# Expert products on 32-column quarters of the TensorE array, gated rows turned by VectorE

## The chip, the core and the metric

The kernel runs on one core of a Trainium2 chip. The metric is the device time of one execution in microseconds (us), as the median of several runs; lower is better. TensorE is the matrix engine, VectorE, ScalarE and GpSimd (POOL) work on tiles in on-chip memory (SBUF) and in the accumulator memory (PSUM), and SyncE (SP) mostly issues transfers (DMA). All tensors here are float32.

## What is computed

A decoder of two layers over 2 x 2048 tokens of width 512: attention, cross-attention and a quantised feed-forward block, then a convolution layer, a cross-attention and a mixture of experts. The change concerns the last part, whose reference is

```python
x = inputs.reshape(b * s, e)                       # 4096 tokens, e = 512
gate_logits = jnp.einsum('te,ex->tx', x, gate_kernel)
weights, selected = jax.lax.top_k(gate_logits, TOP_K)     # 2 of 64 experts
weights = jax.nn.softmax(weights, axis=-1)
...
h0 = jax.lax.ragged_dot(sorted_x, w0, group_sizes)  # w0, w1: 64 x 512 x 1024
h1 = jax.lax.ragged_dot(sorted_x, w1, group_sizes)
inter = jax.nn.silu(h0) * h1
out_sorted = jax.lax.ragged_dot(inter, wo, group_sizes)   # wo: 64 x 1024 x 512
...
out = jnp.einsum('BKE,BK->BE', per_tok, weights)
```

Its result is added to the residual stream.

## The kernel before

The stages run one after the other; the last is `stage_experts` (L3233). The stage before it sorts the 8192 pairs of a token and an expert into tiles of G = 64 tokens with one expert each (partly filled where an expert's count is not a multiple of 64; some experts have no tile), and writes tables of the tokens of each tile and of the expert of each tile. The number of tiles is known only at run time, so each engine runs a loop `Fori` over four tiles (`rounds`, L3269 and after), with the last four tiles behind it. All engines meet by semaphores; nothing but the order written in each engine's block sets the order of its work.

Per tile c:

- SP (`load`) brings each expert's w0, w1 and wo (2 MB each) into a shelf of NBUF = 2 experts. The load of expert e waits until the last tile of expert e - 2 has taken its weights from the shelf, and SP issues the loads strictly in the order w0, w1, wo.
- VectorE `place` (L3376) copies w0 and w1 of the tile's expert from the shelf to `w_s[0]`, `w_s[1]`, ScalarE's `place` (L3425) copies wo to `w_s[2]`, for every tile. There is one such buffer for each, so a copy waits for the product of the tile before that reads it.
- ScalarE fetches the tile's token numbers (`st.fetch`, six small DMAs), VectorE makes indexes of them (L3358), POOL gathers the rows of x by indirect DMA (L3322), and VectorE turns them in 32x32 blocks into `xT`, 128 partitions x 4 blocks of the width x 64 tokens (`turn_x`, L3363).
- TensorE `up(c, p, which)` (L3474) multiplies with w0 (which = 0) or w1 (which = 1). A tile of 64 tokens is the stationary operand, 128 x 64, so one product fills half of the array's columns. The 1024 output columns are cut in Q = 2 halves of FQ = 512; half q goes to partitions q * 64 and after of PSUM bank `which`, for KD = 4 blocks of the width. So the two halves of the array work on the two halves of the output.
- ScalarE `silu` (L3430) makes g of bank 0, VectorE `gate` (L3382) multiplies it with bank 1 to h (128 x 512).
- TensorE `turn_h` (L3481) turns h by four transposes of 128x128 into bank 2, and ScalarE `keep_h` (L3435) copies it to `hT`.
- TensorE `down` (L3490) multiplies hT with wo: FC = 8 blocks, Q = 2 halves of DQ = 256 columns, into bank 4. VectorE scales the result by the token's weight (`y`, L3409), and POOL adds it to the output by indirect DMA (L3339).

The order on TensorE is up(c+1, w0), turn_h(c), up(c+1, w1), down(c). The order on VectorE is, for tile c: output index and weight, index(c+3), turn_x(c+2), place w0 (c+2), gate(c+1), place w1 (c+2), y(c). On ScalarE: fetch(c+4), silu(c+1), keep_h(c), place wo (c+1). xT, g, h and hT are double buffers.

In the traces each float32 matmul with a full stationary operand shows as two records of a weight load and a matmul.

Of the kernel before, what the change touches and what calls it, by code (L numbers as in the profile page):

```python
# [12 lines left out]
P = 128  # L13
# [2826 lines left out]
G = 64  # L2840
# [392 lines left out]
def stage_experts(nc, st, xn_d, table, out_d):  # L3233

    XH = G // LANES
    HJ = FQ // P
    FC = FF // P
    NS = NSLOT
    ident, part, own, shelf, consts_in, w_in = st.ident, st.part, st.own, st.shelf, st.consts_in, st.w_in
    raw, raw_in, raw_x, raw_x_in, entry, own_in = st.raw, st.raw_in, st.raw_x, st.raw_x_in, st.entry, st.own_in  # L3240
    with st:
# [6 lines left out]
        xT = st.sb("xT", [P, 2, KD, G])  # L3248
        g = st.sb("g", [P, 2, FQ])
        h = st.sb("h", [P, 2, FQ])  # L3250
        hT = st.sb("hT", [P, 2, FC, G])
        y = st.sb("y", [P, 4, DQ])
# [7 lines left out]
        h_done = st.count("h_done", 1)  # L3260
        t_mm = st.count("t_mm", 1)
        hT_done = st.count("hT_done", 1)
# [85 lines left out]
        def _(dve):  # L3348
            for s in (w_set[0], w_set[1], ix_done, out_set, xT_done, h_done, y_done):
                s.start(dve)  # L3350
# [27 lines left out]
            def gate(c, p):  # L3378
                dve.wait_ge(*g_done(c))
                dve.wait_ge(*up_mm[1](c))  # L3380
                dve.wait_ge(*t_mm(c - 2))
                dve.tensor_tensor(h[:, p % 2], g[:, p % 2], ps[:, 1, 0:FQ], ALU.mult).then_inc(h_done.sem, 1)  # L3382

            def first():
                for c in range(3):
                    index(0, c, c)
                for c in range(2):
                    turn_x(0, c, c)
                for c in range(2):
                    e, buf = owner(dve, c)  # L3390
                    for n in range(2):
                        place(n, c, e, buf)
                gate(0, 0)

            def main(i, c, p, left):
                aim(i, c, p)
                if left >= 3:
                    index(i + 1 if p else i, c + 3, (p + 3) % 4)
                if left >= 2:
                    turn_x(i + 1 if p >= 2 else i, c + 2, (p + 2) % 4)  # L3400
                    e, buf = owner(dve, c + 2)
                    place(0, c + 2, e, buf)
                if left >= 1:
                    gate(c + 1, p + 1)
                if left >= 2:
                    place(1, c + 2, e, buf)
                dve.wait_ge(*y_mm(c))
                dve.wait_ge(*out_set(c))
                dve.tensor_scalar(y[:, p, :], ps[:, 4, 0:DQ], wt[:, p:p + 1], None, ALU.mult).then_inc(y_done.sem, 1)  # L3409
# [4 lines left out]
        def _(act):  # L3414
            for s in (w_set[2], g_done, hT_done):
                s.start(act)
# [10 lines left out]
            def silu(c, p):  # L3427
                act.wait_ge(*up_mm[0](c))
                act.wait_ge(*h_done(c - 2))
                act.activation(g[:, p % 2], ps[:, 0, 0:FQ], ACT.Silu).then_inc(g_done.sem, 1)  # L3430

            def keep_h(c, p):
                act.wait_ge(*t_mm(c))
                act.wait_ge(*y_mm(c - 2))
                act.activation(hT[:, p % 2].rearrange("p (q j) t -> p j q t", j=HJ),  # L3435
                               ps[:, 2, 0:HJ * P].rearrange("p (j q t) -> p j q t", j=HJ, q=Q), ACT.Copy).then_inc(hT_done.sem, 1)

# [6 lines left out]
            def main(i, c, p, left):  # L3444
# [6 lines left out]
                if left >= 1:  # L3451
                    silu(c + 1, p + 1)
                keep_h(c, p)
                if left >= 1:
                    place(c + 1)
# [4 lines left out]
        def _(pe):  # L3460
            for s in (up_mm[0], up_mm[1], t_mm, y_mm):
                s.start(pe)
# [5 lines left out]
            def up(c, p, which):  # L3468
                pe.wait_ge(*w_set[which](c))
                pe.wait_ge(*xT_done(c))  # L3470
                pe.wait_ge(*(g_done, h_done)[which](c - 1))
                for k in range(KD):
                    for q in range(Q):
                        mm = pe.matmul(ps[q * G:(q + 1) * G, which, 0:FQ], xT[:, p % 2, k, :], wu[which][:, k, q * FQ:(q + 1) * FQ], start=k == 0, stop=k == KD - 1)  # L3474
                mm.then_inc(up_mm[which].sem, 1)

            def turn_h(c, p):
                pe.wait_ge(*h_done(c))
                pe.wait_ge(*hT_done(c - 1))
                for j in range(HJ):  # L3480
                    mm = pe.transpose(ps[:, 2, j * P:(j + 1) * P], h[:, p % 2, j * P:(j + 1) * P], ident[:, :])  # L3481
                mm.then_inc(t_mm.sem, 1)

            def down(c, p):
# [3 lines left out]
                for k in range(FC):  # L3488
                    for q in range(Q):
                        mm = pe.matmul(ps[q * G:(q + 1) * G, 4, 0:DQ], hT[:, p % 2, k, :], wd[:, k, q * DQ:(q + 1) * DQ], start=k == 0, stop=k == FC - 1)  # L3490
                mm.then_inc(y_mm.sem, 1)
# [5 lines left out]
            def main(i, c, p, left):  # L3497
                if left >= 1:
                    up(c + 1, p + 1, 0)
                turn_h(c, p)  # L3500
                if left >= 1:
                    up(c + 1, p + 1, 1)
# [64 lines left out]
def laid_out(inputs):  # L3567
# [8 lines left out]
    for n in ("L0_ffn_qweights", "L0_ffn_scales", "L0_ffn_lora_b"):  # L3576
        t[n] = t[n].transpose(0, 2, 1)
    t.update(shape_constants())
    return {n: np.ascontiguousarray(v) for n, v in t.items()}
# [13 lines left out]
```

## Time and profile before

| | |
|---|---|
| median of 3 runs | 5372.88 us (5367.45 to 5378.44) |
| span of the profiled execution | 5339.0 us |
| TensorE busy in it | 5071.4 us, 95%, 26,624 matmul records and as many weight loads |
| VectorE busy | 2763.7 us, 52% |
| ScalarE busy | 1731.5 us, 32% |
| POOL busy | 1689.6 us, 32% |
| granted TensorE clock, mean | 0.980 of full speed |

The span goes from the first to the last instruction of the profiled execution; the device time of a run holds some time ahead of it and behind it as well. The busy shares are means over stages with different limits. The expert stage begins at about 3460 us and lasts to the end. The views used below are: a table of busy times by stretch, one line's instructions, the chain of waits (the work that ended last, followed back from the end, printed in order of time), groups of instructions by line, and timelines. PE is TensorE's matmuls, PEld its weight loads, DVE VectorE, ACT ScalarE. "128*64 128x256" means a stationary operand of 128 rows and 64 columns and a moving one of 128 x 256.

### The profile page before, as it was taken

How to read it: one execution, taken by the hardware profiler on the slowest of the kernel's cores; microseconds unless marked ns; L12 is line 12 of the kernel's file. 1: busy time of each engine (PE TensorE's matmuls, PEld its weight loads, DVE VectorE, ACT ScalarE, POOL GpSimd, SP SyncE). 2: the span in 40 equal slices, each digit the busy share in tenths (PEclk: the TensorE clock that was granted, in tenths of full speed). 3: DMA queues.
4: the chain of work that ended last, by engine and by line, in shares of the span. 5: the costliest groups of instructions: out<-in, count | busy, mean ns of one | idle time of the engine just before them, and what ended most of it. 6: DMA issues, size and time to landing. Idle time of an engine off the chain costs nothing. (4 is left out here: it accounts for less than half of the span.)

```text
span 5339.0 us, 79687 instructions
## 1 busy us (share of the span) xinstructions
PE 5071.4 (95%) x26624; PEld 2768.0 (52%) x26624; DVE 2763.7 (52%) x4714; ACT 1731.5 (32%) x2238; POOL 1689.6 (32%) x1428
## 2 busy tenths in 40 slices
PE   9999989989999999899979999699999999999998
PEld 4444446668886566444444555534444444444444
DVE  4243237766653355455532565555555555555554
ACT  1011015544332200334321443134444444444433
POOL 1000005545553211000012222544444444444443
PEclk9999999989999999999999999899999999999999
DMA  1010021231111233799976022335545667789996
GB/s 58 8 46 10 8 85 48 70 98 32 24 32 64 101 107 132 178 219 211 222 204 218 25 72 77 104 101 150 180 146 185 212 218 250 264 290 332 383 383 233
DMA packets 493432, 771.88 MB, mean 145 GB/s; under 512 B 119505, under 2 KB 263638, under 8 KB 492708
## 3 DMA queue, kind: packets, MB, share of 16 engines
q1 hardware_dynamic: 377072, 723.32, 42.1%
q0 software_dynamic: 36160, 43.09, 4.1%
q10 hardware_dynamic: 79988, 2.67, 1.0%
q8 instruction: 129, 2.11, 0.2%
q14 instruction: 83, 0.68, 0.0%
HBM read 577.15 MB, written 116.26 MB: 130 GB/s over the span
## 5 line engine op out<-in xcount | busy, mean ns | idle before, releaser
L3474 PE MATMUL ex_ps<-ex_w,ex_xT 128*64 128x512 f32 x5248 | 1193.0, 597 | 13.3 <-DVE ex_w L3376 11.6
L3376 DVE COPY ex_w<-ex_shelf 128x4096 f32 x328 | 753.6, 2298 | 369.0 <-PE ex_ps L3474 235.1
L3425 ACT ACTIVATE ex_w<-ex_shelf 128x4096 f32 x164 | 593.4, 3618 | 888.8 <-PE ex_ps L3490 769.6
L3474 PEld LDWEIGHTS ex_ps<-ex_w,ex_xT 128*64 128x64 f32 x5248 | 366.7, 137 | 625.6 <-issue 588.7
L3490 PE MATMUL ex_ps<-ex_w,ex_hT 128*64 128x256 f32 x5248 | 596.9, 380 | 26.6 <-issue 22.7
L3322 POOL DMA_INDIRECT ex_x<-moe_xn,ex_ix x328 | 556.8, 1698 | 132.2 <-issue 98.7
L3339 POOL DMA_INDIRECT out<-ex_y,ex_ix_out x164 | 293.2, 1788 | 896.9 <-DVE ex_xT L3363 407.7
L3490 PEld LDWEIGHTS ex_ps<-ex_w,ex_hT 128*64 128x64 f32 x5248 | 384.1, 137 | 283.6 <-issue 120.3
L2766 POOL TENSOR_TENSOR go_xb<-go_xr,go_bias 128x2048 f32<-128x2048 f32 x8 | 38.2, 4774 | 719.5 <-DMA go_xr<-x 653.2
L3382 DVE TENSOR_TENSOR ex_h<-ex_g,ex_ps 128x512 f32<-128x512 f32 x164 | 112.6, 686 | 252.3 <-PE ex_ps L3474 214.9
L617 PE MATMUL at_ps<-at_xT,at_kT 128*128 128x512 f32 (+3 forms) x640 | 239.3, 529 | 1.6 <-ACT at_kT L511 1.6
L617 PEld LDWEIGHTS at_ps<-at_xT,at_kT 128*128 128x128 f32 x640 | 117.0, 191 | 121.5 <-issue 108.9
L1760 ACT ACTIVATE ff_gT<-ff_ps,ff_bet,ff_gam 128x128 f32<-128x128 f32 x384 | 137.5, 484 | 120.7 <-PE ff_ps L1803 120.6
L2631 PE MATMUL cv_ps<-cv_xin,cv_split 128*128 128x512 f32 x320 | 157.5, 633 | 17.8 <-ACT cv_g L2520 9.5
L3430 ACT ACTIVATE ex_g<-ex_ps 128x512 f32<-128x512 f32 x164 | 97.9, 597 | 232.9 <-issue 232.9
L2652 PE MATMUL cv_ps<-cv_gt,cv_fwd 128*64 128x256 f32 x1280 | 157.0, 389 | 7.9 <-DMA cv_gt<-cv_g 7.9
L1744 ACT ACTIVATE ff_y<-ff_y,ff_nm,ff_rs 128x512 f32<-128x512 f32 x96 | 72.9, 808 | 268.7 <-POOL ff_nm L1460 268.7
L2587 DVE TENSOR_TENSOR cv_m<-cv_z,cv_hat 128x512 f32<-128x512 f32 x128 | 79.9, 687 | 150.1 <-ACT cv_z L2545 149.6
L891 POOL TENSOR_TENSOR xb_s<-xb_s,xb_rec 128x616 f32<-128x616 f32 x64 | 78.0, 1218 | 233.0 <-DVE xb_rec L961 231.9
L575 PE MATMUL at_ps<-at_v,at_low 128*128 128x512 f32 x336 | 146.8, 593 | 0.0
L2520 ACT ACTIVATE cv_g<-cv_ps 128x512 f32<-128x512 f32 x160 | 94.8, 599 | 144.8 <-PE cv_ps L2631 144.8
L2198 PE MATMUL pr_ps<-pr_t,pr_s 128*128 128x384 f32 x384 | 137.3, 491 | 4.1 <-DVE pr_t L2121 2.5
(360 smaller groups left out, 8130.5 us busy)
## 6 DMA issues: line engine op xcount, KB each, us to landing
ex_shelf<-L_ffn_w SPq DMA_DIRECT2D x128, 2048.0 KB, 13.9
ex_shelf<-L_ffn_wo SPq DMA_DIRECT2D x64, 2048.0 KB
cv_gt<-cv_g SPq DMA_DIRECT2D x320, 128.0 KB, 3.8
cv_vt<-cv_v SPq DMA_DIRECT2D x256, 128.0 KB, 5.2
ff_x<-x SPq DMA_DIRECT2D x16, 1024.0 KB, 7.2
ex_raw_x<-slot_token ACTq DMA_DIRECT2D x656, 0.5 KB
at_low<-x SPq DMA_DIRECT2D x8, 1024.0 KB, 7.4
x<-at_acc SPq DMA_DIRECT2D x8, 1024.0 KB, 4.2
```

The costliest lines, as they stand in the source:

```text
L575: i = pe.matmul(ps[:, 4 + n % 4, :], prob[g][:, j % 4, (it - 4 * g) * P:(it - 4 * g + 1) * P], v[:, j, :], start=j == js[0], stop=j == js[-1])
L617: i = pe.matmul(ps[:, bank + ic - origin // CH, lo - ic * CH:], kT[:, k, j * P:(j + 1) * P], xT[:, k, lo:(ic + 1) * CH], start=k == 0, sto ...
L1760: i = act.activation(gT[:, k, j * P:(j + 1) * P], ps[:, side_bank(("g", s, j)), k * P:(k + 1) * P], ACT.Gelu, bias=bet[:, b, k:k + 1], sca ...
L2198: i = pe.matmul(bank[:, 0:NPC], lhs[:, k], rhs[:, k], start=first and k == 0, stop=k == HK - 1, skip_group_check=not first)
L2631: i = pe.matmul(bank, split[:, u // 4, :], rows, start=True, stop=True)
L2652: i = pe.matmul(ps[o * RT:(o + 1) * RT, z_bank(n, q) + ri, u * CW:(u + 1) * CW], fwd[:, r, ri, :], gt[:, n % 2, r, :], start=True, stop=True)
L3322: pool.indirect_dma_start(out=x[:, p, h, :], out_offset=None, in_=xn_q, in_offset=bass.IndirectOffsetOnAxis(ap=ix[:, p, h:h + 1], axis=0)) ...
L3339: pool.indirect_dma_start(out=out_q, out_offset=bass.IndirectOffsetOnAxis(ap=ix_out[:, p:p + 1], axis=0), in_=y[:, p, :], in_offset=None, ...
L3376: dve.tensor_copy(w_s[n][:, :], pick(shelf[n], buf)).then_inc(w_set[n].sem, 1)
L3425: act.activation(w_s[2][:, :], pick(shelf[2], buf), ACT.Copy).then_inc(w_set[2].sem, 1)
L3474: mm = pe.matmul(ps[q * G:(q + 1) * G, which, 0:FQ], xT[:, p % 2, k, :], wu[which][:, k, q * FQ:(q + 1) * FQ], start=k == 0, stop=k == KD - 1)
L3490: mm = pe.matmul(ps[q * G:(q + 1) * G, 4, 0:DQ], hT[:, p % 2, k, :], wd[:, k, q * DQ:(q + 1) * DQ], start=k == 0, stop=k == FC - 1)
```

## The change

The stationary operand is now half a tile, 32 tokens, and a product runs on four quarters of 32 array columns. In `up`, for each half hh of the tile and each k, quarter r multiplies with a quarter of the output, FL = 256 columns. So a bank holds in partitions r * 32 and after the 32 tokens, and in its free dimension (hh, 256 columns). In `down`, quarter r = q * 2 + hh takes output half q and token half hh. The columns of w0 and w1 are laid out beforehand so that column block r of 256 holds, for each of the 8 blocks k of 128, its 32 columns r * 32 and after; then a transpose of 32x32 blocks brings every element of h to the partition where wo has its row. This transpose is one VectorE instruction (`turn_h`, now in VectorE's block behind `gate`, waiting for h and for down(c-2)). TensorE's four transposes, bank 2 and ScalarE's `keep_h` are gone, and the counter `t_mm` with them; `gate` waits for the transpose of c-2 in its place.

```diff
@@ stage_experts
-    HJ = FQ // P
     FC = FF // P
+    FL = FF // QUADS
...
+    hT = st.sb("hT", [P, 2, FC, XH, LANES])
...
             def gate(c, p):
                 dve.wait_ge(*g_done(c))
                 dve.wait_ge(*up_mm[1](c))
-                dve.wait_ge(*t_mm(c - 2))
-                dve.tensor_tensor(h[:, p % 2], g[:, p % 2], ps[:, 1, 0:FQ], ALU.mult).then_inc(h_done.sem, 1)
+                dve.wait_ge(*hT_done(c - 2))
+                dve.tensor_tensor(h[:, p % 2], g[:, p % 2], ps[:, 1, :], ALU.mult).then_inc(h_done.sem, 1)
+
+            def turn_h(c, p):
+                dve.wait_ge(*h_done(c))
+                dve.wait_ge(*y_mm(c - 2))
+                dve.transpose(hT[:, p % 2].rearrange("p k h j -> p h k j"),
+                              h[:, p % 2].rearrange("p (h k i) -> p h k i", h=XH, k=FC)).then_inc(hT_done.sem, 1)
...
                 if left >= 1:
                     gate(c + 1, p + 1)
+                    turn_h(c + 1, p + 1)
...
-            def keep_h(c, p):
-                act.wait_ge(*t_mm(c))
-                act.wait_ge(*y_mm(c - 2))
-                act.activation(hT[:, p % 2].rearrange("p (q j) t -> p j q t", j=HJ),
...
                 if left >= 1:
                     silu(c + 1, p + 1)
-                keep_h(c, p)
-                if left >= 1:
                     place(c + 1)
...
-                for k in range(KD):
-                    for q in range(Q):
-                        mm = pe.matmul(ps[q * G:(q + 1) * G, which, 0:FQ], xT[:, p % 2, k, :], wu[which][:, k, q * FQ:(q + 1) * FQ], start=k == 0, stop=k == KD - 1)
+                for hh in range(XH):
+                    for k in range(KD):
+                        for r in range(QUADS):
+                            mm = pe.matmul(ps[r * LANES:(r + 1) * LANES, which, hh * FL:(hh + 1) * FL], xT[:, p % 2, k, hh * LANES:(hh + 1) * LANES],
+                                           wu[which][:, k, r * FL:(r + 1) * FL], start=k == 0, stop=k == KD - 1)
...
                 for k in range(FC):
                     for q in range(Q):
-                        mm = pe.matmul(ps[q * G:(q + 1) * G, 4, 0:DQ], hT[:, p % 2, k, :], wd[:, k, q * DQ:(q + 1) * DQ], start=k == 0, stop=k == FC - 1)
+                        for hh in range(XH):
+                            r = q * XH + hh
+                            mm = pe.matmul(ps[r * LANES:(r + 1) * LANES, 4, 0:DQ], hT[:, p % 2, k, hh, :], wd[:, k, q * DQ:(q + 1) * DQ], start=k == 0, stop=k == FC - 1)
...
             def main(i, c, p, left):
                 if left >= 1:
                     up(c + 1, p + 1, 0)
-                turn_h(c, p)
-                if left >= 1:
                     up(c + 1, p + 1, 1)
                 down(c, p)
@@ laid_out
+    for n in ("L1_ffn_w0", "L1_ffn_w1"):
+        t[n] = t[n].reshape(NE, D, FF // P, QUADS, LANES).transpose(0, 1, 3, 2, 4).reshape(NE, D, FF)
```

On TensorE, in the expert loop, a tile stood in the row as follows before (`ex_ps` are the PSUM banks, `ex_w` the placed weights, `ex_ident` the identity of the transposes):

```order
L3474 MATMUL ex_ps<-ex_w,ex_xT 64x512 x8
L3479 REGISTER_ALU
L3481 MATMUL ex_ps<-ex_ident,ex_h 128x128 x4
L3474 MATMUL ex_ps<-ex_w,ex_xT 64x512 x8
L3490 MATMUL ex_ps<-ex_w,ex_hT 64x256 x16
```

and stands there now:

```order
L3474 MATMUL ex_ps<-ex_w,ex_xT 32x256 x64
L3481 REGISTER_ALU
L3486 MATMUL ex_ps<-ex_w,ex_hT 32x256 x32
```

The transposes between the two up products have gone, the two up products follow each other, and there are 96 matmuls where there were 32 and 4 transposes.

On VectorE, in the same loop, from the copy of w0 to the scaling of y, before:

```order
L3376 COPY ex_w<-ex_shelf 128x4096
L3382 TENSOR_TENSOR ex_h<-ex_g,ex_ps 128x512
L3376 REGISTER_ALU
L3376 COPY ex_w<-ex_shelf 128x4096
L3408 ISA
L3409 TENSOR_SCALAR ex_y<-ex_ps,ex_wt 128x256
```

and now:

```order
L3375 COPY ex_w<-ex_shelf 128x4096
L3381 TENSOR_TENSOR ex_h<-ex_g,ex_ps 128x512
L3386 STREAM_TRANSPOSE ex_hT<-ex_h 128x2x8x32
L3375 REGISTER_ALU
L3375 COPY ex_w<-ex_shelf 128x4096
L3415 ISA
L3416 TENSOR_SCALAR ex_y<-ex_ps,ex_wt 128x256
```

The transpose stands between the gate and the copy of w1; all else keeps its place.

## Rows read from the trace of the kernel before

**Rows 1.** Table by stretch, core 0: busy us (instructions), clock, DMA share, GB/s.

```profile
3500.00:4890.00 1390.00, 1382.42 (x8492) 619.00 (x8490) 802.38 (x1001) 588.03 (x375) 652.27 (x375) 1.00 0.64 202
4890.00:5240.00 350.00, 334.84 (x2052) 153.89 (x2050) 192.12 (x241) 141.12 (x90) 155.35 (x90) 1.00 1.05 383
5240.00:5339.00 99.00, 84.37 (x522) 39.28 (x518) 40.87 (x55) 36.68 (x23) 33.25 (x20) 0.95 0.56 181
```

**Rows 2.** One line's instructions, L3409, in the same three stretches: ns min/median/max.

```profile
L3409 DVE TENSOR_SCALAR ex_y<-ex_ps,ex_wt x125: 477/484/486, 3500.9 to 4881.0; 128x256 f32<-128x256 f32 x125
...
L3409 DVE TENSOR_SCALAR ex_y<-ex_ps,ex_wt x30: 466/483/485, 4892.1 to 5231.4; 128x256 f32<-128x256 f32 x30
...
L3409 DVE TENSOR_SCALAR ex_y<-ex_ps,ex_wt x9: 483/484/486, 5241.2 to 5328.3; 128x256 f32<-128x256 f32 x9
```

**Rows 3.** Chain of waits in order of time, first stretch: start us, us, what.

```profile
4103.37 3.45 PE ex_ps L3490 x32
4106.82 3.43 PE ex_ps L3474 x16
4110.25 0.59 PE ex_ps L3481 x4
4110.84 3.58 PE ex_ps L3474 x16
```

**Rows 4.** The same chain in the second stretch.

```profile
4922.47 3.67 PE ex_ps L3490 x32
...
4992.51 3.67 PE ex_ps L3490 x32
```

**Rows 5.** Groups by line and shape, from 3200 us on: busy us, mean ns, idle before.

```profile
L3490 PEld LDWEIGHTS ex_ps<-ex_w,ex_hT 128*64 128x64 f32 x5248 | 384.1, 137 | 283.6 <-issue 120.3 <-ACT ex_w L3425 4.0
...
L3363 DVE STREAM_TRANSPOSE ex_xT<-ex_x 128x256 f32<-128x256 f32 x164 | 72.4, 441 | 67.8 <-DMA ex_x<-moe_xn,ex_ix 67.6
```

**Rows 6.** L1146 in the attention stage: timeline, its instructions (ns), table of a stretch.

```profile
3052.47 0.64 PE L1146 MATMUL xb_ps<-xb_pT,xb_v 77*32 77x128 f32 x16
...
L1146 PEld LDWEIGHTS xb_ps<-xb_pT,xb_v x32: 107/110/111, 3052.5 to 3058.7; 77*32 77x32 f32 x32
L1146 PE MATMUL xb_ps<-xb_pT,xb_v x32: 272/273/298, 3052.5 to 3058.8; 77*32 77x128 f32 x32
...
938.70:942.65 3.95, 3.95 (x58) 3.04 (x57) 3.79 (x7) 3.03 (x4) 2.40 (x2) 1.00 0.00 0
```

**Rows 7.** Timeline of VectorE in the first stretch: start us, us, what, idle before.

```profile
4210.03 2.29 DVE L3376 COPY ex_w<-ex_shelf 128x4096 f32 x1 [2.15 <-PE ex_ps L3474]
4214.05 0.69 DVE L3382 TENSOR_TENSOR ex_h<-ex_g,ex_ps 128x512 f32<-128x512 f32 x1 [1.72 <-PE ex_ps L3474]
...
4217.55 0.48 DVE L3409 TENSOR_SCALAR ex_y<-ex_ps,ex_wt 128x256 f32<-128x256 f32 x1 [0.61 <-PE ex_ps L3490]
```

**Rows 8.** Chain of waits around an expert without a tile.

```profile
3732.40 3.48 PE ex_ps L3490 x32
...
3736.05 3.63 ACT ex_w L3425
...
3740.01 11.55 DMA ex_shelf<-L_ffn_wo
...
3757.09 3.67 PE ex_ps L3490 x32
...
3654.78 3.67 PE ex_ps L3490 x32
...
3859.87 3.67 PE ex_ps L3490 x32
```

**Rows 9.** DMA queues: of the whole span (first row), and from 3540 to 5280 us.

```profile
q8 instruction: 129, 2.11, 0.2%
...
q14 instruction: 1, 0.01, 0.0%
...
ex_raw<-slot_token ACTq DMA_DIRECT2D x310, 0.5 KB, 5.5
```

More of the change, by code:

```diff
@@ L3248, in stage_experts @@
         xT = st.sb("xT", [P, 2, KD, G])
-        g = st.sb("g", [P, 2, FQ])
-        h = st.sb("h", [P, 2, FQ])
-        hT = st.sb("hT", [P, 2, FC, G])
+        g = st.sb("g", [P, 2, XH * FL])
+        h = st.sb("h", [P, 2, XH * FL])
+        hT = st.sb("hT", [P, 2, FC, XH, LANES])
         y = st.sb("y", [P, 4, DQ])
@@ L3260, in stage_experts @@
         h_done = st.count("h_done", 1)
-        t_mm = st.count("t_mm", 1)
         hT_done = st.count("hT_done", 1)
@@ L3348, in _ @@
         def _(dve):
-            for s in (w_set[0], w_set[1], ix_done, out_set, xT_done, h_done, y_done):
+            for s in (w_set[0], w_set[1], ix_done, out_set, xT_done, h_done, hT_done, y_done):
                 s.start(dve)
@@ L3393, in first @@
                 gate(0, 0)
+                turn_h(0, 0)
             def main(i, c, p, left):
@@ L3414, in _ @@
         def _(act):
-            for s in (w_set[2], g_done, hT_done):
+            for s in (w_set[2], g_done):
                 s.start(act)
@@ L3429, in silu @@
                 act.wait_ge(*h_done(c - 2))
-                act.activation(g[:, p % 2], ps[:, 0, 0:FQ], ACT.Silu).then_inc(g_done.sem, 1)
-            def keep_h(c, p):
-                act.wait_ge(*t_mm(c))
-                act.wait_ge(*y_mm(c - 2))
-                act.activation(hT[:, p % 2].rearrange("p (q j) t -> p j q t", j=HJ),
-                               ps[:, 2, 0:HJ * P].rearrange("p (j q t) -> p j q t", j=HJ, q=Q), ACT.Copy).then_inc(hT_done.sem, 1)
+                act.activation(g[:, p % 2], ps[:, 0, :], ACT.Silu).then_inc(g_done.sem, 1)
             def first():
@@ L3460, in _ @@
         def _(pe):
-            for s in (up_mm[0], up_mm[1], t_mm, y_mm):
+            for s in (up_mm[0], up_mm[1], y_mm):
                 s.start(pe)
@@ L3471, in up @@
                 pe.wait_ge(*(g_done, h_done)[which](c - 1))
-                for k in range(KD):
-                    for q in range(Q):
-                        mm = pe.matmul(ps[q * G:(q + 1) * G, which, 0:FQ], xT[:, p % 2, k, :], wu[which][:, k, q * FQ:(q + 1) * FQ], start=k == 0, stop=k == KD - 1)
-                mm.then_inc(up_mm[which].sem, 1)
[L3477 to L3482, printed above, removed]
+                for hh in range(XH):
[3 more added lines that the diff above has]
+                                           wu[which][:, k, r * FL:(r + 1) * FL], start=k == 0, stop=k == KD - 1)
+                mm.then_inc(up_mm[which].sem, 1)
             def down(c, p):
```

## The prediction

> **What bounds the kernel now.** I read the last two fifths of the span, since the change touches only the experts, and cut them into three stretches [rows 1]. [...] From 4890 to 5240 us TensorE is busy 335 of 350 us, and now the DMA share is 1.05 at 383 GB/s: this stretch goes at the pace at which expert weights arrive. [...] The products scaled by L3409 count the tiles in these stretches: 125, 30 and 9, together 164 [rows 2].
>
> Inside the first stretch the chain of waits is nothing but TensorE [rows 3]: one tile is down product 3.45 us, up product with w0 3.43, turn of h 0.59, up product with w1 3.58, then the next down product. The sum is 11.05 us, with no waiting row between them. The second up product is 0.15 us longer than the first, although it has the same 16 instructions: the records restart there, behind the turn. In the second stretch every third down product comes behind a gap, as at 4922.47 and, six tiles later, at 4992.51 us [rows 4]: 35.0 us for three tiles, where TensorE's own work is 3 x 11.05 = 33.2. So a faster tile gains nothing there unless DMA gets faster too. 350 us at 35.0 us is ten such groups, the 30 tiles of [rows 2].
>
> **The turn leaves TensorE.** Removed from each tile are the 0.59 us of the turn and the 0.15 us by which the product behind it is late: 0.74 us. ScalarE loses the copy of h from PSUM; no row of the chain is that copy [rows 3], so it counts nothing.
>
> **The products themselves.** Before, an up product is 8 matmuls of 512 columns on two 64-column halves, after it 32 of 256 columns on four 32-column quarters; each matmul is two records. In streamed columns per lane that is 16 x 512 / 2 = 4096 against 64 x 256 / 4 = 4096. The down product goes from 32 x 256 / 2 to 64 x 256 / 4, again 4096. So everything hangs on whether four quarters stream at once as two halves do. The halves: 32 records of the down product take 3.45 us start to start, 0.216 us for a pair of 256 columns, that is 0.108 per 128 columns. The nearest row for quarters is L1146: 16 records of 32 columns of weights and 128 moving columns in 0.64 us, one of them 0.273 us long [rows 6]. Taking off the last record leaves (0.64 - 0.273) / 3 = 0.12 us for a group of four, the first one after a restart included. Two at a time would have needed 8 groups, about 1.0 us. So quarters do run four wide, at 0.108 to 0.12 us per 128 columns. I take 0.108, because the excess sits in the restart, which the experts no longer have between products. A product is then 16 groups x 0.216 = 3.45 us, and a tile 3 x 3.45 = **10.35 us**, against 11.05: 0.70 us less. (Taking 0.74 off 11.05 gives 10.31; the difference is rounding of the rows.) Bounds: 10.29 (3 x 3.43) and 11.5 (3 x 16 x 2 x 0.12, every group at L1146's mean), which is above the 11.05 of now; the third rival takes up that end.
>
> The weight loads double in number and halve in width; a load of 64 columns took 137 ns and one of 32 columns 110 ns [rows 5, 6]. A quarter has its next load hidden under its own 0.216 us group. If a load stuck out, 48 groups would each pay; the 110 ns would have to double first.
>
> **The turn on VectorE.** A transpose of 128x256 took 441 ns [rows 5]. For 128x512 the bounds are 0.69 us (the gate's multiplication of 512 elements [rows 7]) and 0.88 (twice 441 ns); I take 0.71, near the other 512-element instruction. It stands between the gate and the copy of w1, and queued behind it are this copy, the scaling of y, and, through y, the index for the gather and ScalarE's six small fetches. By [rows 7] VectorE waits 2.15 us for TensorE ahead of the w0 copy and 1.72 ahead of the gate, and 0.61 ahead of y. After up w1 ends it now does gate 0.69, turn 0.71, copy 2.29, plus about 0.3 of gaps: 4.0 us. TensorE has down and up w0 ahead of it, 6.9 us, before it wants the new w1: 2.9 us to spare. The scaling of y comes about 0.5 us later; its bank is wanted 6.9 us after down. VectorE's load per tile is 802 / 1390 x 11.05 = 6.4 us now [rows 1], then (6.4 + 0.71) / 10.35 = 69%. hT is wanted a whole up w0 + up w1 after it could be ready. ScalarE's copy of w2, 3.63 us [rows 8], starts behind down and has 6.9 us. Cost on the path: **0**. If that cover were gone, the full 0.71 us per tile would show, the gain of the change. The gathers, the small fetches and the stores keep their queues; their order on POOL, SP and ScalarE does not change.
>
> **Where a faster tile meets DMA.** Early on w2 of an expert is late in three places, where the expert ahead of it seems to have no tile: copy at 3736.05, load issued at 3740.01, landed after 11.55 us, copied by ScalarE, down product at 3757.09 [rows 8]. From the down product at 3732.40 the unhindered one would be at 3732.40 + 2 x 11.05 = 3754.5, so 2.6 us are lost; with tiles of 10.35 it is 4.0. Three such places, the down products at 3654.78, 3757.09 and 3859.87 [rows 8], cost 3 x 1.4 = 4 us. In the first stretch the loads have room: where two experts have four tiles these took 44.2 us and will take 41.4, while two experts' weights need 35.0 at full DMA rate [rows 4].
>
> **The sum.** (125 + 9) tiles x 0.70 = 94 us, less 4, is 90. The profiled execution's span is 5339.0 us; the median of the three runs, 5372.9, is 33.9 more, the start and end around the span, which the change leaves alone. 5339 - 90 + 34 = **5283 us**.
>
> **Rivals.**
> - *Instructions fetched again* (0.17). The loop over four tiles goes from 4 x 136 = 544 loads and matmuls to 1536. The instruction queue q8 moved 129 blocks in the whole span and none from 3540 to 5280 us [rows 9]; the program's 53,248 loads and matmuls less 39 repeats of 544 make 32,000, 248 to a block. So a loop of 2.2 blocks is held now; whether one of 6.2 blocks is, no row shows. If not, each pass waits at least for the block behind its branch. Bounds from nothing (the queue ahead covers it) to 5.5 us (the small loads' time to landing [rows 9]); I take 2.5, times 31 passes outside the DMA stretch: 78 us back, **5361**. [...]
> - *Issue rate, slower* (0.10). TensorE must start 384 records in 10.35 us, one per 27 ns, where it starts one per 81 now. The densest long stretch has 58 + 57 records in 3.95 us, one per 34 ns [rows 6]; there the array was busy throughout, which speaks against issue being its limit, and 16 matmuls with 16 loads in 0.64 us go faster still. It decides from 28.8 ns (11.05 / 384). At 34 ns a tile takes 13.1 us: 134 x 2.05 = 275, and the DMA stretch grows by 10 x (39.3 - 35.0) = 43: **5691**.
> - *Quarters overlap badly with 128 rows* (0.05). L1146 has 77 rows and bursts of 4 groups only. [...]
> - *The DMA stretch gains too* (0.05): if its pace hangs on tiles rather than on bandwidth, 164 x 0.70 = 115 us, **5258**. The share of 1.05 speaks against it.
> - *Small waits on VectorE* (0.05): POOL's gather or y a little late, 0.2 to 0.4 us a tile, **5310 to 5340**.
> - The forecast, 5265 to 5300, has 0.58.
>
> **Range and signs.** 5255 to 5362 holds the forecast, the gain in the DMA stretch, the small waits and two thirds of the refetch case (up to 2.5 us a pass): 0.58 + 0.05 + 0.05 + 0.11 = 0.79. These are also the cases that are faster by over 0.2% (10.7 us, about what a measurement of this kernel can tell from no change). Within 0.2%: 0.03 of the refetch case. Slower: the other 0.03 of it, 0.10 and 0.05, 0.18.
>
> **What would show it.** Right: in the chain of the first stretch three rows of 64 records each, 3.45 us apart, no waiting row; matmuls of 32x256 at 0.054 us each in busy time; the DMA stretch still 35 us for three tiles; no q8 blocks in the loop; VectorE's 128x512 transpose near 0.71 us. Wrong: groups of four more than 0.23 us apart; TensorE idle once per four tiles beside q8 packets; "issue" as what ends TensorE's waits; w1's copy ahead of an up product in the chain.

## The result, and the profile after

The changed kernel takes **5285.5 us** (median, 5280.0 to 5295.4) where the kernel before takes 5370.6 in the same group of runs: 0.9845 of it, 95% interval 0.9833 to 0.9857, 85 us faster. The forecast was 5283. In a later group, where the kernel before takes 5343.7 us, the changed kernel takes 5249.6, which is 94 us less (0.9816, 0.9800 to 0.9832). The sum of the prediction, 90 us, lies between the two.

The page of the changed kernel, its first part and the groups of the expert stage (line, engine, operation, tiles, shape, count | busy us, mean ns of one | idle before, and what ended it):

```profile
span 5281.0 us, 120235 instructions
...
PE 5001.8 (95%) x46960; PEld 3484.6 (66%) x46960; DVE 2866.6 (54%) x4878; ACT 1653.9 (31%) x2074; POOL 1695.1 (32%) x1428
...
q8 instruction: 137, 2.24, 0.2%
...
L3474 PE MATMUL ex_ps<-ex_w,ex_xT 128*32 128x256 f32 x20992 | 1223.1, 380 | 32.0 <-DVE ex_w L3375 27.2
L3474 PEld LDWEIGHTS ex_ps<-ex_w,ex_xT 128*32 128x32 f32 x20992 | 1033.6, 110 | 168.1 <-DVE ex_w L3375 33.4
...
L3486 PE MATMUL ex_ps<-ex_w,ex_hT 128*32 128x256 f32 x10496 | 652.0, 380 | 11.1 <-ACT ex_w L3432 7.0
```

One load of 32 columns is 110 ns, as L1146 had it [rows 6]. In the table by stretch, the three stages answer to [rows 1] (busy us and instructions of PE, PEld, DVE, ACT, POOL, then clock, DMA share, GB/s):

```profile
3520.00:4830.00 1310.00, 1304.83 (x24037) 1182.63 (x24033) 883.09 (x1130) 527.16 (x250) 655.40 (x375) 1.00 0.67 215
4830.00:5180.00 350.00, 331.33 (x5805) 260.35 (x5800) 210.06 (x272) 127.74 (x61) 156.74 (x91) 1.00 1.05 383
5180.00:5281.00 101.00, 85.54 (x1512) 74.01 (x1504) 50.34 (x66) 33.53 (x16) 39.28 (x22) 0.94 0.61 205
```

The first stage holds the same 125 tiles, now in some 1310 to 1357 us by where it is cut, with TensorE again busy nearly throughout. The second is what it was: 30 tiles in 350 us at 383 GB/s. A steady tile in the chain of waits, which answers to [rows 3] (start us, us, what):

```profile
4116.55 0.12 PE ex_ps L3486 x3
4116.77 3.24 PE ex_ps L3486 x60
4120.00 0.12 PE ex_ps L3474 x3
4120.22 6.69 PE ex_ps L3474 x124
4126.91 0.12 PE ex_ps L3486 x3
```

From 4116.55 to 4126.91 is 10.36 us: the turn's row between the two up products is gone, and the 128 records of both run as one piece but for their ends. No waiting row stands between them.

For all that follows I also counted the starts of ScalarE's 164 silus in each trace. They cut the stage at the same tiles in every kernel, wherever it lies in its span:

| profiled execution | first silu at | silus 0-40 | 40-127 | 127-157 | 157-163 | to the end |
|---|---|---|---|---|---|---|
| before (5339.0) | 3488.9 | 446.0 | 962.0 | 349.4 | 64.9 | 27.9 |
| changed (5281.0) | 3517.9 | 419.7 | 905.0 | 349.3 | 62.3 | 26.7 |
| changed again (5248.4) | 3493.3 | 417.1 | 901.3 | 349.2 | 60.8 | 26.6 |

87 tiles from silu 40 to 127 go from 11.06 us each to 10.36 (10.40 in the first profile); from 127 to 157 nothing goes.

### The profile page after: what moved, and what is told of

It reads as the page before. It is cut to its first block and busy times, and to the rows that moved or that the text cites. A ratio compares the mean times of both kernels' runs of the same rounds, so it can differ in the third digit from the quotient of the medians.

```text
span 5281.0 us, 120235 instructions
## 1 busy us (share of the span) xinstructions
PE 5001.8 (95%) x46960; PEld 3484.6 (66%) x46960; DVE 2866.6 (54%) x4878; ACT 1653.9 (31%) x2074; POOL 1695.1 (32%) x1428
## 5 line engine op out<-in xcount | busy, mean ns | idle before, releaser
L3474 PE MATMUL ex_ps<-ex_w,ex_xT 128*32 128x256 f32 x20992 | 1223.1, 380 | 32.0 <-DVE ex_w L3375 27.2
L3474 PEld LDWEIGHTS ex_ps<-ex_w,ex_xT 128*32 128x32 f32 x20992 | 1033.6, 110 | 168.1 <-DVE ex_w L3375 33.4
L3486 PE MATMUL ex_ps<-ex_w,ex_hT 128*32 128x256 f32 x10496 | 652.0, 380 | 11.1 <-ACT ex_w L3432 7.0
L3486 PEld LDWEIGHTS ex_ps<-ex_w,ex_hT 128*32 128x32 f32 x10496 | 524.5, 110 | 84.4 <-issue 18.5
L3362 DVE STREAM_TRANSPOSE ex_xT<-ex_x 128x256 f32<-128x256 f32 x164 | 72.7, 443 | 124.1 <-DMA ex_x<-moe_xn,ex_ix 122.7
```

The costliest lines, as they stand in the source:

```text
L3474: mm = pe.matmul(ps[r * LANES:(r + 1) * LANES, which, hh * FL:(hh + 1) * FL], xT[:, p % 2, k, hh * LANES:(hh + 1) * LANES], wu[which][:, k ...
L3486: mm = pe.matmul(ps[r * LANES:(r + 1) * LANES, 4, 0:DQ], hT[:, p % 2, k, hh, :], wd[:, k, q * DQ:(q + 1) * DQ], start=k == 0, stop=k == FC ...
```

## The experiments

Times of one experiment are compared with the kernel before of its own group: 5344.3 us for the first four kernels, 5369.9 for the next four, 5343.7 for the last four. Each of these groups ran on a chip of its own; for the group of the result no chip is on record, and its kernel before took 5370.6.

### Whose gain is it: the narrow tiles' or the turn's?

Two kernels do one half of the change each. Both leave the values of the product in another order than the next product wants; the work of every engine is otherwise that of the kernels that they stand between.

Halves, with the turn on VectorE (`up` is shown; `down` goes back to halves in the same way):

```diff
-                for hh in range(XH):
-                    for k in range(KD):
-                        for r in range(QUADS):
-                            mm = pe.matmul(ps[r * LANES:(r + 1) * LANES, which, hh * FL:(hh + 1) * FL], ...
+                for k in range(KD):
+                    for q in range(Q):
+                        mm = pe.matmul(ps[q * G:(q + 1) * G, which, 0:FQ], xT[:, p % 2, k, :], ...
```

> The changed kernel with its up and down products back on two array tiles of 64 columns, while the turn of the gated rows stays on VectorE. The values of h land in another order than w1's rows, so the output is another one; the work of each engine is that of halves with the turn off TensorE. My theory, that the gain is TensorE's time for the turn and the restart behind it, and that halves and quarters take the same time for the same columns: a tile takes 10.31 to 10.36 us and the kernel 5285 us, within 10. The rival, that the four narrow tiles bring the gain: a tile stays near 11 us and the kernel near 5371 us. If both share it, the time lies between and the two tile times say how much is whose.

Quarters, with the turn on TensorE and its copy on ScalarE (the reverse edit, made on the kernel before):

> The kernel before with its up and down products on four array tiles of 32 columns, while the turn stays on TensorE and its copy on ScalarE. The rows of the product land in another order, so the output is another one. My theory: a tile stays at 11.05 to 11.1 us and the kernel at 5371 us, within 8, since four quarters take the time of two halves. The rival, that the narrow tiles bring the gain: 5285 us.

Measured: halves with the turn on VectorE 5249.2 us (0.9813, 0.9797 to 0.9830), quarters with the turn on TensorE 5347.4 us (1.0007, 0.9997 to 1.0016). The first takes the whole gain, the second none of it. The chain of the first, the halves:

```profile
4105.86 6.87 PE ex_ps L3473 x32
4112.73 3.45 PE ex_ps L3482 x32
4116.18 6.87 PE ex_ps L3473 x32
```

and of the second, the quarters with the turn between:

```profile
4114.22 0.59 PE ex_ps L3484 x4
4114.81 3.59 PE ex_ps L3476 x64
4118.40 3.45 PE ex_ps L3495 x64
4121.85 3.45 PE ex_ps L3476 x64
4125.31 0.59 PE ex_ps L3484 x4
```

A tile is 10.32 us in the one and 11.09 in the other. A down product is 3.45 us whether it is 32 records of 64 columns or 64 of 32. So the gain is TensorE's 0.59 us for the turn and the 0.14 us of the restart behind it, and the quarters are there to make VectorE's turn possible: they put the same tokens on all four groups of 32 partitions, which a turn in 32x32 blocks needs. With halves a turn in blocks would leave two groups of tokens in the same columns, which the next product can't use; so that kernel is no version to keep.

The first of the two had gaps of 0.04 to 0.07 us a tile in its favour, and I had only compared it over groups, so both ran once more in one group, unchanged:

> The changed kernel once more, on the same chip as the halves kernel below it. The kernel before took 5344 us in one group of runs and 5370 in another, so the experiments are compared within a group. I expect 0.984 to 0.986 of the kernel before, and that the first tile of the experts begins at another time than in the other profiled executions while the stage from there on takes the same 1736 us, within 3.

> The kernel with halves of 64 columns and the turn on VectorE once more (values of h in another order than w1's rows). The first run gave a steady ten tiles in 103.2 us where the changed kernel takes 103.9, and 1726.8 us from the first silu to the last where the changed kernel takes 1736.4. If the four narrow tiles cost a little on TensorE (0.05 to 0.07 us for each tile), this kernel is 7 to 10 us faster than the changed one on the same chip. The rival, that the difference came from waits that vary between executions: within 4 us of it.

Measured: the changed kernel 5249.6 us (0.9816, 0.9800 to 0.9832), the halves 5250.9 (0.9823, 0.9808 to 0.9839). I had expected the halves to be 7 to 10 us faster; they are not, though their 87 middle tiles take 898.4 us in the trace where the changed kernel's take 901.3. The traces put a quarter's cost over a half at 0.03 to 0.04 us a tile, which the times can't tell from nothing. The changed kernel's silus span 1728.5 us here, not 1736 within 3 as I had expected: 8 us of the stage differ between its two profiles.

### How much room has VectorE?

The changed kernel, with one or three more turns of the same size into a tile that nobody reads:

```diff
+                for again in range(n):
+                    dve.transpose(spare[:, again].rearrange("p (k h j) -> p h k j", k=FC, h=XH),
+                                  h[:, p % 2].rearrange("p (h k i) -> p h k i", h=XH, k=FC))
                 dve.transpose(hT[:, p % 2].rearrange("p k h j -> p h k j"),
                               h[:, p % 2].rearrange("p (h k i) -> p h k i", h=XH, k=FC)).then_inc(hT_done.sem, 1)
```

> The changed kernel with one more VectorE transpose of 128x512 for each tile, into a tile that nobody reads: 0.71 us more on VectorE between the gate and the w1 copy's consumer. The prediction's spare of 2.9 us on VectorE says 5285 us, no change. A sum round the loop that I made since, from the y product through the fetch, silu, gate, turn and back (9.2 us of the 10.36 of a tile), also says no change, with 0.45 us left. The rival, that the turn has no cover: 134 x 0.71 = 95 us more, 5380 us.

> The changed kernel with three more VectorE transposes of 128x512 for each tile, into a tile that nobody reads: 2.13 us more on VectorE. The prediction's spare of 2.9 us says no change, 5285 us. The sum round the loop (9.2 us + 2.13 = 11.3 against 10.36) says 0.95 us more for each tile, 134 x 0.95 = 127 us if the stretch that waits for the weights pays too and 104 x 0.95 = 99 us if it does not: 5385 to 5413 us. No cover at all: 134 x 2.13 = 285 us, 5571 us.

Measured: one more turn 5251.2 us (0.9820, 0.9804 to 0.9837), 1.5 above the changed kernel in the other group with the same time before; three more 5334.9 us (0.9980, 0.9971 to 0.9990), which is 85 us above and gives nearly the whole gain back; the ring's sum in the expectation said 99 to 127. The row of the turn in the changed kernel, and VectorE and ScalarE over one tile of the kernel with three more (timeline: start us, us, what, idle before):

```profile
L3386 DVE STREAM_TRANSPOSE ex_hT<-ex_h x164: 711/711/715, 3519.6 to 5258.4; 128x512 f32<-128x512 f32 x164
```

```profile
4423.59 0.69 DVE L3382 TENSOR_TENSOR ex_h<-ex_g,ex_ps 128x512 f32<-128x512 f32 x1 [1.45 <-ACT ex_g L3441]
4424.31 1.90 DVE L3388 STREAM_TRANSPOSE ex_spare<-ex_h 128x512 f32<-128x512 f32 x3
4426.13 0.67 DVE L3390 STREAM_TRANSPOSE ex_hT<-ex_h 128x512 f32<-128x512 f32 x1
4426.72 2.25 DVE L3376 COPY ex_w<-ex_shelf 128x4096 f32 x1
4428.90 0.47 DVE L3420 TENSOR_SCALAR ex_y<-ex_ps,ex_wt 128x256 f32<-128x256 f32 x1
...
4430.58 1.77 ACTq L3225 DMA_DIRECT2D ex_raw_x<-slot_token  x4
4432.44 1.12 ACTq L3227 DMA_DIRECT2D ex_raw<-slot_token  x2
4433.75 0.60 ACT L3441 ACTIVATE ex_g<-ex_ps 128x512 f32<-128x512 f32 x1 [5.06 <-issue]
```

Read it as a ring: gate, turns, w1 copy, y, then ScalarE's six fetches (which wait for VectorE's index and weights), then its silu, then the next gate. Between the silu at 4422.96 (not shown) and the one at 4433.75 lie 10.79 us, more than TensorE's 10.36. In the changed kernel the same ring sums to some 9.2 us, so it is hidden; three turns in a row take 1.90 us, not three times 0.71. The sum 9.2 + 1.9 = 11.1 meets the mean of the 87 middle tiles (963.9 us, 11.08 each), but in part by chance: a quarter of these tiles take 10.7 us or less and the median is 10.85, while others take up to 12.6, so the ring by itself is nearer 10.7 and the mean holds other waits that the ring no longer hides. The spare on VectorE is therefore an estimate, 1.2 us a tile by the sum and some 1.5 by the shorter tiles. The prediction's 2.9 would have covered these 1.9 and is ruled out. That it is this ring which sets the pace is read from the rows and from the semaphores in the code; no run shortened it at another place. With one more turn (9.8 to 9.9) the middle tiles took 10.49 in the trace, a first trace of the ring, but that execution was the slowest of its four (5258.9 us), and the median shows nothing.

### Does the stretch at DMA's pace hold the rest back?

From the third expert on, only half of each expert's weights is loaded (`whole` is true for the first two alone):

```diff
-        sp.dma_start(st.shelf[n][:, b].rearrange("p (k n) -> p k n", k=src.shape[1] // P),
-                     src_e.rearrange("o (k p) n -> p (o k) n", p=P)).then_inc(st.w_in[n], 16)
+        part = k if whole else k // 2
+        sp.dma_start(st.shelf[n][:, b].rearrange("p (k n) -> p k n", k=k)[:, 0:part, :],
+                     src_e.rearrange("o (k p) n -> p (o k) n", p=P)[:, 0:part, :]).then_inc(st.w_in[n], 16)
```

> The kernel before, where from the third expert on only half of each expert's weights is loaded (the rest of the buffer keeps older values, so the results differ; the instructions of the engines are the same). It shows what the stretch in which the weights' transfers set the pace costs the kernel before. My theory: the 30 tiles of that stretch go from 35.0 us for three to 3 x 11.05, which is 18 us less, and the three bubbles behind experts without a tile fall away, 8 us: 5345 us, within 8.

> The changed kernel with the same half loads. My theory: the 30 tiles go from 35.0 us for three to 3 x 10.36, 39 us less, and the bubbles give back 12 us: 5234 us, within 8; against the kernel before with half loads that is 111 to 115 us, not 85, since the stretch now yields its 30 x 0.70 and the bubbles' 4 too. The rival, that something other than the loads keeps that stretch at its pace: the difference stays at 85 us.

Measured: 5341.5 us for the kernel before with half loads (0.9941, 0.9922 to 0.9960) and 5232.0 for the changed one (0.9744, 0.9724 to 0.9763): 109.5 us apart where whole loads leave 85 in the group of the result; the sum had said 111 to 115. The second stretch of the changed kernel with half loads:

```profile
4830.00:5130.00 300.00, 299.73 (x5531) 274.78 (x5527) 202.54 (x259) 122.44 (x58) 152.65 (x87) 1.00 0.73 225
```

TensorE is busy all through and the DMA share falls from 1.05 to 0.73. Silus 127 to 157 take 312.6 us in place of 349.3. With whole loads this stretch withholds 37 us from the changed kernel. It gains nothing from faster tiles, as the chain with whole loads says, one load behind the other:

```profile
4913.20 18.11 DMA ex_shelf<-L_ffn_w
...
4931.44 16.55 DMA ex_shelf<-L_ffn_w
```

The three bubbles are seen here too: silus 0 to 40 lose 8.8 us to whole loads in the kernel before (446.0 - 437.2) and 9.4 in the changed one (419.7 - 410.3), or 6.8 by its second profile (417.1 - 410.3).

I tried to get these 37 us by another order of the experts:

```diff
-            step(dve.tensor_scalar(fold, rank_c, -2.0, float(2 * NE - 1), ALU.mult, ALU.add))
-            step(dve.scalar_tensor_tensor(pos, rank_c, 2.0, fold, ALU.mult, ALU.min))
+            step(dve.tensor_scalar(fold, rank_c, -1.0, float(NE - 1), ALU.mult, ALU.add))
+            step(dve.tensor_tensor(pos, rank_c, fold, ALU.min))
+            step(dve.tensor_scalar(fold, pos, -2.0, float(NE - 1), ALU.mult, ALU.add))
+            step(dve.scalar_tensor_tensor(pos, pos, 2.0, fold, ALU.mult, ALU.min))
+            step(dve.tensor_scalar(fold, rank_c, NE / 2 - 0.5, None, ALU.is_gt))
+            step(dve.scalar_tensor_tensor(pos, pos, 2.0, fold, ALU.mult, ALU.add))
```

> The changed kernel with another order of the experts: the ten pairs of experts that have three tiles between them, now in one row at the end, are put between pairs that have more tiles. My theory: a pair takes 35.0 us of loads, three tiles take 31.1 us, and with longer pairs between them the loads run ahead by enough, so that 10 x 3.9 = 39 us go: 5247 us, 5240 to 5260. The rival, that the loads' waits only move: 5285 us.

Measured: 5300.3 us (0.9863, 0.9844 to 0.9883), 15 above the changed kernel's 5285.5 in the group of the result, whose kernel before took the same time: worse than the rival. The late stretch is free now, silus 127 to 157 take 317.3 us, but the 127 tiles before them take 50 us more. The table by stretch of this kernel:

```profile
3525.00:4850.00 1325.00, 1293.94 (x23395) 1092.84 (x23395) 853.72 (x1099) 512.70 (x245) 626.53 (x365) 1.00 0.72 236
4850.00:5200.00 350.00, 346.97 (x6348) 317.27 (x6346) 233.95 (x299) 139.22 (x66) 167.37 (x100) 1.00 0.89 301
```

and what VectorE waits for ahead of its copies of w0 and w1, from 3800 to 5200 us (us in total, times, longest):

```profile
DVE ex_w L3379 <- DMA ex_shelf<-L_ffn_w: 112.3, 40, 8.1
```

In the changed kernel the same row has 87.4 us in 35 times, the longest 4.9.

My theory had the loads run ahead while a long expert computes. They can't: there are two shelves, and a load starts when the expert two places earlier has been copied for its last time. In this order three short experts stand in a row between two long ones, and each such row waits for its loads while the time of the long expert before them went unused, as the starts of the loads show (four within 53 us, 3647.3 to 3700.0, then none until 3790.1). The order with one long and one short expert in turn is the better one. The rows carry only part of the 50 us: TensorE's own waits from 3525 to 4850 us sum to 28 us, and the rest is not accounted for, so this cause is argued more than shown.

### Is the longer loop held?

TensorE's loop body covers eight or six tiles in place of four; the other engines are unchanged:

```diff
-            rounds(pe, first, main)
+            first()
+            with pe.Fori(0, 20) as i:
+                for p in range(8):
+                    main(i, i * 8 + p, p, 4)
+            for p in range(4):
+                main(40, 160 + p, p, 3 - p)
```

> The changed kernel with TensorE's loop body covering eight tiles instead of four, with half as many passes; the other engines are unchanged. The loop then holds some 12.4 blocks of instructions instead of 6.2. If a loop of that length is no longer held, the instruction queue fetches some 12 blocks in each pass, some 240 in the loop. My theory: they come ahead of time and cost nothing, 5285 us, within 6. The rival of the prediction, with the stall that it priced at 2.5 us for each pass: some 40 us more, 5325 us.

> The changed kernel with TensorE's loop body covering six tiles, 26 passes: some 9.3 blocks of instructions where four tiles have 6.2 and eight have 12.4. The loop of eight fetched 272 more blocks and cost about 100 us, a stall of some 5 us at each pass. If a loop of 9.3 blocks is not held either, it fetches some 9 to 10 blocks a pass, about 250 in all, and stalls 26 times 5 us, 130 us: about 5415 us where the changed kernel takes 5285. If it is held: no block in the loop and 5285 us, within 6 (each against a kernel before of 5370).

The same eight tiles on the kernel before, whose tiles have 136 records and not 384:

> The kernel before with TensorE's loop body covering eight tiles: some 4.4 blocks of instructions, since a tile has 136 matmuls and weight loads there, not 384. If the length in blocks is what counts: no block in the loop and the time of the kernel before, within 5 us. The rival, that a loop of eight tiles costs by itself (branch, waits): some 100 us more.

Measured: the loop of eight 5389.0 us (1.0035, 1.0026 to 1.0045), 103.5 above the changed kernel in the group of the result, whose kernel before took the same time. The loop of six 5395.2 us (1.0088, 1.0069 to 1.0106), 145.6 above the changed kernel of its own group. The kernel before with a loop of eight 5344.9 (1.0005, 0.9995 to 1.0015), no difference. So my theory, that the blocks come ahead of time and cost nothing, was wrong, and the rival's 2.5 us a pass too low. The instruction queue from 3540 to 5200 us, in the changed kernel with its loop of four, then with the loop of eight, then of six (packets, MB, share), and the kernel before with a loop of eight:

```profile
q8 instruction: 3, 0.05, 0.0%
```

```profile
q8 instruction: 255, 4.18, 1.0%
```

```profile
q8 instruction: 262, 4.29, 1.0%
```

```profile
q8 instruction: 2, 0.03, 0.0%
```

The 3 and the 2 blocks of the first and the last are fetched before 3600 us; from 3600 to 5200 us both fetch none. What TensorE waited for, from 3520 to 5200 us: the changed kernel, the loop of eight, the loop of six:

```profile
PE ex_ps L3474 <- DVE ex_w L3375: 14.8, 12, 2.3
...
PE ex_ps L3474 <- issue: 0.9, 4, 0.3
```

```profile
PE ex_ps L3474 <- issue: 62.9, 23, 6.2
PE ex_ps L3474 <- DVE ex_xT L3362: 13.2, 5, 3.9
```

```profile
PE ex_ps L3474 <- issue: 91.2, 28, 6.0
PE ex_ps L3474 <- DVE ex_xT L3362: 16.9, 4, 5.3
```

"issue" is a wait for nothing that the profile shows, here some 3 us a pass, and up to 6.2. The whole cost is 103.5 / 20 = 5.2 us a pass, and 145.6 / 26 = 5.6. Of that the rows give 3 to 3.5 as issue and 0.7 as waits for VectorE's xT, which the changed kernel did not have. Most of the rest is TensorE's clock. A branch of the loop of eight, as TensorE's row (start us, us, what, idle before) and by stretch:

```profile
4417.24 9.35 PE L3474 MATMUL ex_ps<-ex_w,ex_xT 128*32 128x256 f32 x128 [5.02 <-issue]
```

```profile
4415.00:4421.80 6.80, 4.56 (x44) 2.20 (x48) 0.35 (x1) 1.03 (x1) 3.00 (x3) 0.50 1.05 350
```

TensorE stood idle for 5.02 us, the granted clock fell to 0.50 for 6.8 us, and the next down product began at 4426.40, so these two up products took 9.16 us where they take 6.91 at 1.00. From 3520 to 5200 us the clock fell so 16 times in the loop of eight and 23 times in the loop of six, for 3.4 or 6.8 us each, and never in the first profile of the changed kernel. In the loop of eight the two up products behind such a branch took 1.7 to 2.9 us more, 33.5 us in all or 1.7 a pass, and with the 62.9 and 13.2 us of the rows this is 110 us for the 103.5 measured. The row puts all 5.02 us down to issue, but at this branch VectorE's xT was late too, done at 4415.37, 1.9 us before TensorE began. The cost goes with the number of passes, not of blocks: both loops fetch nearly the same number.

So the loop that fetches again is real, and its edge lies between 6.2 blocks (held, 102 KB at the 16.4 KB a block of the row with 4.18 MB in 255) and 9.3 (not held, 152 KB). These lengths are estimates from 248 records a block: over the whole span the two loops fetched 409 and 421 blocks, 272 and 284 more than the changed kernel's 137, 13.6 and 10.9 a pass, 1.2 and 1.6 above the estimates. The stall is there at 9.3 and 12.4 blocks; the loop of 6.2 fetched nothing from 3600 to 5200 us. Where between 6.2 and 9.3 the edge lies, and what sets it, is not shown.

## Why the prediction was right, step by step

- **The products.** Groups of four at 0.216 us, a product at 3.45, a tile at 10.35: measured 3.45 and 10.36. The reading of L1146 as four wide [rows 6] held; the kernels with one half of the change each show that halves and quarters take the same time (3.45 us a down product in both).
- **The turn leaves TensorE, 0.70 us a tile.** Between silus 40 and 127: 962.0 to 901.3 us, 87 tiles, 0.70 each. In the first profile of the changed kernel it is 0.66 (905.0 us), though TensorE waits 0.5 us in all in those tiles. Its weight loads wait 3.5 us there in 10 places for nothing that the profile shows (`PEld ex_ps L3474 <- issue`), and not at all in the second profile, which is about these 3.7 us. What made them, and why the gain was 85 us in one group and 94 in the other, stays open. The sum counts the nine tiles behind the DMA stretch at 0.70 as well: from silu 157 to 163 six tiles went from 64.9 us to 62.3 in the first profile and 60.8 in the second, 0.43 and 0.68 a tile.
- **The turn on VectorE.** 0.711 us, forecast 0.71, cost on the path 0. Right in its result, but the reason was too generous: it looked only at how long TensorE can do without the new w1 (2.9 us), and not at the ring through y, the fetches, silu and gate, whose room is some 1.2 to 1.5 us. A turn at 0.88, the upper bound, or one more small step would still have fitted; 1.9 us more did not, and cost 85 us.
- **The DMA stretch gains nothing.** 349.4 to 349.3 us. With half loads it does gain, 332.2 to 312.6. Right, by the cause given.
- **Bubbles, 3 x 1.4 = 4 us.** Mis-sized: against half loads they cost 8.8 us in the kernel before and 9.4 or 6.8 after, by the two profiles, so between 0.6 more and 2.0 less, and not 4 more. In the trace the copy and the load that made the w2 late ran as follows, where [rows 8] had 3736.05 and 3757.09:

```profile
3746.78 3.29 PE ex_ps L3486 x61
...
3750.42 3.65 ACT ex_w L3432
...
3754.40 11.03 DMA ex_shelf<-L_ffn_wo
...
3765.64 3.63 ACT ex_w L3432
3769.31 3.66 PE ex_ps L3486 x64
```

  Two tiles after the down product that began near 3746.7 would be 3767.4; it came 1.9 us later, not 4.0. The load landed after 11.03 us, not 11.55, and the rest is a term that the forecast carried over: in the kernel before, TensorE started only 1.69 us after the copy of w2 had ended, with no releaser that the profile shows,

```profile
3755.41 1.69 issue
3757.09 3.67 PE ex_ps L3490 x32
```

  while in the changed kernel it starts 0.04 us after the copy. So 4.0 less 1.7 less 0.5 gives the 1.9. Why that start was late before, no run here shows. The loads of w0 and w1 are late at these places as well, and their share is in the 8.8, 9.4 and 6.8.
- **"33.9 us around the span."** Wrong, though the total did not suffer. Only 2 us lie around a span (5282.99 against 5281.0). The profiled execution of before, with its span of 5339.0, belongs with the groups where the kernel takes 5344 us; the three times of before belong with those where it takes 5370. Most of the difference is in the routing stage ahead of the experts. First load of the experts (duration ns, first and last start), the changed kernel in the group of the result and again in the last group:

```profile
L3211 SPq DMA_DIRECT2D ex_shelf<-L_ffn_w x128: 175/382/2807, 3491.3 to 5211.1; - x128
```

```profile
L3211 SPq DMA_DIRECT2D ex_shelf<-L_ffn_w x128: 372/382/2806, 3466.7 to 5179.7; - x128
```

  The kernel before starts them at 3462.3 in its profile; with half loads, in the second group of experiments, at 3490.9. In the routing stage of the changed kernel's first profile, 3364 to 3491 us, stands a wait that the second has not:

```profile
DVE ro_m L3012 <- DMA moe_xn<-xb_xn_o: 15.9, 2, 11.0
```

  All five profiles of the groups at 5370 have this row, with 12.8 to 19.1 us, and none of the nine at 5344. Its releaser is the profile's guess: in the code this instruction waits only for semaphores of TensorE, VectorE and ScalarE, and from 3364 to 3490 us TensorE's granted clock is lower too, 0.68 against 0.77. So where the time goes is shown and its cause is not. The subtraction of 90 from the median was right all the same, because most of the difference falls in a stage that the change leaves alone. That the forecast is within 3 us is in part luck: its time before was 2.3 us too high (5372.9 for 5370.6) and its gain 5 us too large (90 for 85).
- **The rivals.** Instructions fetched again did not happen at 6.2 blocks, but it was mis-priced: a pass costs 5.2 to 5.6 us, not 2.5, and 40 passes would have cost 208 to 224 us, a kernel near 5500 by that estimate. The range, which ended at 5362 and was to hold two thirds of this case, would not have held it. The issue rate is not a limit at 27 ns a record: 384 records ran in 10.36 us. Four tiles of 32 columns with 128 rows do not overlap badly here: the group stayed at 0.216 us, below the 0.230 (11.05 / 48) from which the change would have lost. TensorE's small waits for VectorE (14.8 us in 12 places) lie outside the 87 middle tiles, mostly where the loads set the pace anyway.

## What to carry to other kernels

Moving a small operation off the engine that sets the pace gained its row in the chain plus the restart behind it here (0.59 and 0.14 us a tile); the retiling that makes the move possible must only cost nothing (here 0.03 to 0.04 us a tile by the traces). Before giving an engine more work, sum the ring that leads back to the same instruction one tile later, over every engine in it, and not only the time until its nearest consumer: here the first left some 1.2 to 1.5 us and the second 2.9, and 1.9 us more cost 85. And count a loop's records whenever tiles become narrower: four tiles of 384 are held, six are not, and that costs more (104 and 146 us) than the change brings.

## What the runs showed that I had not expected

- A TensorE loop of 6.2 blocks is held and one of 9.3 is not, and there a pass costs 5.6 us with 10.9 blocks fetched, or 5.2 us with 13.6 in the loop of 12.4. The stall costs twice: TensorE is idle (5.02 us at the branch above), and the granted clock falls to 0.50 for 3.4 or 6.8 us, 16 times in the loop of eight and 23 times in the loop of six.
- Three turns of 128x512 in a row take 1.90 us, 0.63 each, where one shows as 0.71; in the changed kernel too the next instruction starts 0.64 us after the turn (4190.10 to 4190.74 us).
- The same kernel takes 5250 or 5285 us by the group of runs, and 25 us of that lie in the routing stage ahead of the experts. The groups ran on different chips, but none is known to have been used twice, so that the chip makes the difference is likely and not shown.
- Spreading the loads' late stretch over time did not help: with two buffers and three short experts in a row, the tiles before it lost 50 us and the late stretch gave back 32.
- TensorE's late start of 1.69 us behind a late w2 was gone in the changed kernel, so this bubble shrank with the faster tile, from 2.6 us to 1.9, where a sum over the old rows said that it grows to 4.0.
